# Loops of the sixteen-head and local attention stages written out step by step

## The reference, cut to what matters

```python
# layers 0, 1, 3: sixteen heads (layers 0 and 3 turn q and k by position first)
scores = einsum('bhqd,bhkd->bhqk', q, k) * D ** (-0.5)
out = einsum('bhqk,bhkd->bhqd', softmax(scores), v) @ wo + bo
# layer 1, second half, two depths: local attention
sim = einsum('bhwid,bhwjd->bhwij', bq, bk)      # 64 queries against 128 keys
attn = softmax(where(mask, -max, sim)); x = x + einsum('bhwij,bhwjd->bhwid', attn, bv) @ wo
```

## Time and profile before

| what | value |
|---|---|
| median of 3 runs (lowest to highest) | 6350.87 us (6350.7 to 6353.11) |
| the profiled execution's own time | 6336.72 us |
| its span, first to last instruction | 6334.9 us |
| granted TensorE clock, mean over the span | 0.887 |
| PE busy | 5123.1 us (81%) |
| DVE, ACT, POOL busy | 3519.6 (56%), 3125.7 (49%), 2547.7 us (40%) |
| instructions recorded | 118561 |
| DMA packets, bytes | 317744, 313.51 MB |

### The profile page before, as it was taken

The page is one execution under the profiler, slowest core; times in us unless marked ns, Lnnn a source line. Parts: engine busy times, 40 slices in busy tenths (PEclk is TensorE's granted clock), DMA queues, the critical chain, the costliest instruction groups (busy, mean ns, idle before and its releaser), DMA issues. The chain is left out here.

```text
span 6334.9 us, 118561 instructions
## 1 busy us (share of the span) xinstructions
PE 5123.1 (81%) x38207; PEld 2643.1 (42%) x38217; DVE 3519.6 (56%) x5633; ACT 3125.7 (49%) x7068; POOL 2547.7 (40%) x2162
## 2 busy tenths in 40 slices
PE   5999779788885999998799998884226999975995
PEld 2444334233332656563465664353101322232784
DVE  5777432376664656554566664466337988821233
ACT  1666633256563655552365664343012877841542
POOL 3333010222213878761687883105563322116125
PEclk7999989889996999999899999996556999977997
DMA  3344211143320000001000000002102333211123
GB/s 96 101 105 106 57 40 50 43 105 97 94 70 21 6 7 7 8 2 82 19 7 6 6 4 5 2 1 65 34 7 75 90 94 83 74 46 46 54 75 90
DMA packets 317744, 313.51 MB, mean 49 GB/s; under 512 B 85382, under 2 KB 242722, under 8 KB 315298
## 3 DMA queue, kind: packets, MB, share of 16 engines
q1 hardware_dynamic: 300834, 285.80, 16.7%
q0 software_dynamic: 16384, 20.69, 1.2%
HBM read 172.15 MB, written 136.32 MB: 49 GB/s over the span
## 5 line engine op out<-in xcount | busy, mean ns | idle before, releaser
L714 ACT ACTIVATE a_prob<-a_PB 128x512 f32<-128x512 f32 x2304 | 1252.1, 596 | 527.5 <-PE a_PB L590 396.8
L638 PE MATMUL a_PO<-a_prob,a_V 128*32 128x256 f32 (+3 forms) x8192 | 726.9, 428 | 20.1 <-ACT a_cn L687 19.9
L822 DVE TENSOR_REDUCE a_blocks<-a_PA 128x8 f32<-128x1024 f32 x512 | 608.4, 1215 | 137.9 <-PE a_PA L590 137.6
L825 DVE TENSOR_REDUCE a_neg<-a_PA 128x2 f32<-128x1024 f32 x512 | 591.5, 1212 | 52.2 <-PE a_PA L603 52.2
L603 PE MATMUL a_PA<-a_KS,a_QS 48*128 48x512 bf16 (+3 forms) x3072 | 477.1, 350 | 158.5 <-DVE a_blocks L822 44.3
L2409 DVE TENSOR_REDUCE f1a_neg<-f1a_PA 128x2 f32<-128x384 f32 (+1 forms) x512 | 266.6, 521 | 479.2 <-PE f1a_PA L2211 467.0
L2339 POOL TENSOR_TENSOR f1a_prob<-f1a_prob,f1a_inv 128x384 f32<-128x384 f32 (+1 forms) x512 | 394.5, 773 | 318.5 <-DVE f1a_inv L2413 318.4
L620 PE MATMUL a_PB<-a_QS,a_KS 51*128 51x512 bf16 (+3 forms) x3072 | 453.4, 332 | 71.4 <-ACT a_prob L714 42.3
L2303 ACT ACTIVATE f1a_pt<-f1a_PT 128x512 f32<-128x512 f32 (+1 forms) x512 | 278.4, 544 | 361.8 <-PE f1a_PT L2220 358.5
L2296 ACT ACTIVATE f1a_prob<-f1a_PA,f1a_neg 128x192 f32<-128x192 f32 (+1 forms) x1024 | 405.5, 404 | 95.2 <-DVE f1a_neg L2409 95.2
L603 PEld LDWEIGHTS a_PA<-a_KS,a_QS 48*128 48x128 bf16 x3072 | 119.9, 95 | 699.2 <-issue 333.5
(11 more groups left out here) (442 smaller groups left out, 10338.4 us busy)
## 6 DMA issues: line engine op xcount, KB each, us to landing
a_spill<-a_qkp SPq DMA_DIRECT2D x576, 128.0 KB, 2.4
a_QS<-a_spill SPq DMA_DIRECT2D x384, 96.0 KB, 2.6
a_KS<-a_spill SPq DMA_DIRECT2D x384, 96.0 KB, 2.7
a_raw<-a_cn SPq DMA_DIRECT2D x192, 72.0 KB
f_rows<-tokens_in SPq DMA_DIRECT2D x78, 128.0 KB
tokens_out<-f_rows SPq DMA_DIRECT2D x78, 128.0 KB
tokens_in<-f1g_zero SPq DMA_DIRECT2D x9, 1024.0 KB, 13.9
a_heads<-a_raw SPq DMA_DIRECT2D x32, 256.0 KB, 3.3
```

Of the source, the lines that this page charges most:

```text
L638: mm = nc.tensor.matmul(PO[32 * j:32 * j + 32, first:last], V[:, par, t, 8 * e + pr], prob[:, k % st.ring, e, c + first - q0:c + last - q0 ...
L714: nc.scalar.activation(prob[:, k % st.ring, e], PB[:, ring_b.slot(0, ("b", s, e))], ACT.Exp, scale=scale).then_inc(pb_used, 1)
L822: nc.vector.tensor_reduce(to, of, AX, ALU.max).then_inc(pa_used, 1)
L825: nc.vector.tensor_reduce(neg[:, t, pr], PA[:, bank:bank + 2], AX, ALU.max, negate=True).then_inc(pa_used, 1)
```

## The change

Both `steps` functions lose their loop. Each step from the first to the last is written out, on every engine, with `i` a constant. Nothing else is edited; the order of the instructions inside a step stays.

```diff
@@ heads16_phase
         def steps(eng, step):
-            for i in range(FIRST_STEP, 4):
-                step(i, i % 2)
-            with eng.Fori(2, B // 2 - 1) as pair:
-                step(pair * 2, 0)
-                step(pair * 2 + 1, 1)
-            for i in range(B - 2, LAST_STEP + 1):
+            for i in range(FIRST_STEP, LAST_STEP + 1):
                 step(i, i % 2)
@@ local_attention_phase
         def steps(eng, step):
-            for i in (-1, 0, 1):
-                step(i, i % 2)
-            with eng.Fori(1, B // 2 - 1) as pair:
-                step(pair * 2, 0)
-                step(pair * 2 + 1, 1)
-            for i in range(B - 2, B + 1):
+            for i in range(-1, B + 1):
                 step(i, i % 2)
```

## The result

The changed kernel takes 6238.91 us (median of 4 runs, 6225.48 to 6240.31); the kernel before took 6350.78 us in the same rounds (6337.51 to 6353.11). The ratio is 0.9823, with a 95% interval of 0.9808 to 0.9837: 111.9 us less at the medians. The forecast was 6245 us.

What follows compares the result with a forecast made beforehand. TensorE, stopped by long jumps back and then slowed by its clock, was taken to bound the five loops (VectorE next in a3_). Gains 19.7 + 20.2 + 22.1 + 29.0 + 15.3 = 106.3 us off 6350.9 gave 6244.6, range 6225 to 6283.

Steps and rivals of the forecast that it cites:

- clean steps: Five loops: steps with full work and no long jump in or just before them price each loop; gains sum to 106.3 us.
- the direct stalls: TensorE's jumps back in the five loops: medians times taken jumps, together 69.6 us, not the whole price.
- rival 1: Five loops: only direct stalls go, what follows a jump being slack; 69.6 us, so 6281 us; chance 0.11.
- a0_, a3_, f1a_, f1b_: Four loop stages: clean steps of 37.2, 44.6, 48.6 and 48.6 us give gains of 19.7, 22.1, 29.0 and 15.3 us.
- a1_: Sixteen-head loop: ten steps at step 4's 38.5 us, the later and slower one, make 385 us, gain 20.2.
- Rival 2: a1_ keeps its length, set by SP's queue and the wait for the maxima; gain 86.1 us, 6265 us; chance 0.09.
- Waits on constants: TensorE's 4550 wait values at line 36, 250 us of sequencer: removal gains nothing beyond the clean steps, hidden by its queue.
- rival 3: Loops at lines 983 and 2494, moved to other addresses, jump long: 56 us given back, 6301 us; chance 0.04.
- Rival 4: Five written-out stages: straight code is fetched late, about 3.6 us per late block; at 50 late, 6425 us; chance 0.03.
- Rival 5: Five loops: the change does nothing, their length being set by something both forms share; 6351 us; chance 0.04.
- The fetch: TensorE's jumps: the skill's two blocks of 256 or 2048 instructions; the trace fits neither exactly, the sum is the same.
- What would show it: Changed profile: some 106,000 instructions, no TensorE issue idle over 1 us, clock 1.00, steps 37.2, 38.5, 44.6, 48.6 us.

Runs made afterwards that it cites:

- the kernel with the rows first: Changed kernel with SP's six DMAs of the rows of maxima issued ahead of group 2's stacking DMAs: 6177.06 us, ratio 0.9755 to the kernel before.
- TensorE's loops alone: Against the kernel before, only TensorE keeps the five loops; the other four engines have their steps written out: 6295.02 us, ratio 0.9945.
- all but TensorE's: Against the kernel before, only TensorE's steps are written out; the other four engines keep their loops: 6280.49 us, ratio 0.9915.
- the kernel with sixteen heads alone: Against the kernel before, only the sixteen-head stages are written out; both local attention stages keep their loops: 6107.38 us against 6159.44, ratio 0.9917.
- the one with one pass: Against the kernel before, each loop makes one pass, its body holding all ten or twelve steps: 6048.1 us against 6159.44, ratio 0.982.

## Why the prediction was right, and where it wasn't

**Size.** 106.3 us forecast, 112.3 by the stages and 111.9 by the medians. Costing the loops by clean steps in place of stalls is what made it so: the direct stalls of TensorE are 69.6 us (70.5 added jump by jump, since my medians took in the jump that isn't taken), and rival 1, which stopped there, missed by 43.

**a0_, a3_, f1a_, f1b_.** 19.7, 22.1, 29.0 and 15.3 forecast; 20.2, 21.6, 28.3 and 14.6 measured. The steps of a3_ came at 44.65 us in the mean and those of local attention at 48.65, where I had 44.6 and 48.6.

**a1_.** 20.2 forecast, 27.6 measured: 7.4 us, more than the whole miss of the sum. I took step 4's 38.5 us as the later one in a growing series; in the changed kernel the steps don't grow, they go up and down, and the mean of steps 3 and 4, 37.9, would have been right. The reason I gave, SP's queue, is the right limit of this stage, as the kernel with the rows first shows. Rival 2 had the limit right and the consequence wrong: on top of it the jumps still cost 27 us.

**Waits on constants.** This reasoning fell short. I costed them at nothing beyond the clean steps because TensorE's register work hides in its queue. That cover holds in local attention, where TensorE's loops alone make the clean steps 48.4 us. But I looked at TensorE alone. The clean-step terms held the 0.5 us per local step, so the sum was right, and its owners are VectorE and ScalarE: 48.9 to 49.0 and 48.8 us with theirs, 49.4 with all but TensorE's. Why that last one is more than either, when GpSimd and SyncE add nothing alone, is open.

**The owner of the loss.** The prediction gave nearly all room to TensorE's jump and clock, with VectorE's misses as a remark on f1b_. The runs give TensorE 64 us and the others 50. The sum didn't suffer, because clean steps are free of every engine's long jumps, whoever owns them. That f1a_ and f1b_ differ by 13.7 us before was read right as a matter of place, but only on TensorE, and the same holds for VectorE and ScalarE, which miss in opposite stages.

**Rivals 3 and 4.** The loops left alone kept their short jumps, so 3 did not come. (The body at line 983 is a seventh of f1b_'s, not an eighth.) But the kernel with sixteen heads alone did to f1a_ and f1b_ what rival 3 feared for others: 17.5 us given back by a change of place. Rival 3 had the mechanism and not the victim. Rival 4, late fetches of straight code, did not come: the fetches fell from 331 to 303. On TensorE the only idle for "issue" above 1.5 us in the stages is that of the weight loads ahead of the rows of maxima in a1_ (ten, up to 3.2 us), the other face of the wait shown above. Rival 5 is refuted by the result.

**The fetch.** I read the trace as fitting neither 512 nor 2048 instructions in place. The queue of fetches says more: the body stayed in place over two passes, which rules out 512. My count of it, 1412, left out the sequencer's own instructions; with them it is 1705.

**What would show it.** The count of instructions (106,384 against 106,000) and the steps of a3_ and local attention came as named. Four marks missed: the clock of a1_ is 0.97; its steps average 37.8 us and not 38.5; 579 register instructions are not "next to none"; and TensorE's weight loads idle for "issue" over 1 us in a1_ (up to 3.2) and once a step in local attention (1.1). This last is one of the signs that I had named for a wrong forecast: in a1_ it is the wait for the rows, and what it is in local attention, where the steps are as short as forecast, wasn't looked into.

## What to carry to other kernels

Price a loop by steps that ran clean, not by adding up stalls, and look at the jump and the waits of every engine in it, since here 50 of 113 us belonged to engines that the chain of waits hardly named. The length of a jump changed with where the code lay: a body that jumps fast can turn slow by an edit elsewhere, so after any change compare the stages that weren't changed. When the stalls are gone, look at what the steps wait for next; two lines moved in a DMA queue gave a quarter of the whole change again.

## What the runs showed of the hardware

One and the same loop body jumps in 0.2 us or in 3.3 to 5.0 us on TensorE, and in 0.2 to 0.3 or 2.3 to 3.3 us on VectorE and ScalarE. An edit ahead of it in the program changed which, and on TensorE it could also change from pass to pass. In the kernel before and with sixteen heads alone, each of TensorE's long jumps in the five stages had a fetch of 16 KB in it, and no short taken one had. The branch's own record is 40 to 83 ns when it is not taken, or taken on the other engines. The Trainium skill ("Advanced Engine Details and Errata", section "Control Flow Timing") gives about 108 ns for a compare and branch; these rows show less for the record itself, and more until the next instruction runs.

TensorE's clock fell to half after idle stretches of 1.8 to 3.0 us at a DMA just as after those at jumps. So the waits in a1_ cost more than their own length: without them the same work also took 11 us less.

The kernel before took 6159 us in some rounds and 6333 to 6351 in others. In the profiles of the changed kernel and of the one with one pass, which come from either kind, the five stages are the same to 3 us. Over all profiles the difference stands in the slot experts (392 to 394 against 420 to 426 us) and the token experts (531 to 535 against 669 to 689), where one wait of GpSimd for a DMA to `tokens_out` alone is 126.7 against 219.5 us. The cause is open, and kernels are compared only within their rounds.
